# Counts by destination out of the first layer's sums instead of a second histogram

## The reference

```python
x = layernorm(x + segment_sum(x[src], dst, 3125))          # layer 0
x = layernorm(x + ten_steps_of_segment_max(x, w, ...))     # layer 1
# layer 2 needs, for each node, the sum of the weights of its edges, plus one:
deg = segment_sum(concat(edge_weight, ones), concat(edge_dst, arange(n)))
dinv = where(deg > 0, rsqrt(deg), 0)
# layer 3 divides by the number of edges that end in the node:
cnt = segment_sum(ones(E), i_idx); s / maximum(cnt, 1)
```

## Time and profile before

| | us |
|---|---|
| median of 3 runs | 8579.5 |
| the runs | 8568.05, 8579.5, 8579.87 |
| profiled execution, its own time | 8566.12 |
| profiled execution, span of its instructions | 8564.4 |
| DVE busy / PE busy in the span | 6750.9 / 6111.6 |
| mean granted TensorE clock | 0.932 |

### The profile page before, as it was taken

The page is one execution under the profiler, slowest core; times in us unless marked ns, Lnnn a source line. Parts: engine busy times, 40 slices in busy tenths (PEclk is TensorE's granted clock), DMA queues, the critical chain, the costliest instruction groups (busy, mean ns, idle before and its releaser), DMA issues. The chain is left out here.

```text
span 8564.4 us, 139046 instructions
## 1 busy us (share of the span) xinstructions
PE 6111.6 (71%) x42018; PEld 3076.7 (36%) x42018; DVE 6750.9 (79%) x10765; ACT 3629.1 (42%) x4488; POOL 2258.3 (26%) x2014
## 2 busy tenths in 40 slices
PE   2111013878989798888989898989698989656665
PEld 2101012344434343443434343434354545323332
DVE  8999778767889888888889898989787979744443
ACT  0133000224656565555656565656344444233333
POOL 0000000001333333324233332424200000277775
PEclk9999999999999999999999999999899999777777
DMA  2000000886767676666767676767576767311111
GB/s 87 3 0 0 22 5 20 296 286 212 251 211 254 204 244 211 230 227 220 241 214 249 210 251 210 253 204 254 186 285 224 292 225 290 120 22 29 26 29 25
DMA packets 450936, 1460.71 MB, mean 171 GB/s; under 512 B 79869, under 2 KB 115365, under 8 KB 383008
## 3 DMA queue, kind: packets, MB, share of 16 engines
q1 hardware_dynamic: 228922, 1119.71, 38.3%
q10 hardware_dynamic: 157440, 298.89, 9.7%
q0 software_dynamic: 63872, 32.83, 2.2%
HBM read 1159.47 MB, written 291.94 MB: 169 GB/s over the span
## 5 line engine op out<-in xcount | busy, mean ns | idle before, releaser
L1465 PE MATMUL acc<-dst_hot,parts 128*128 128x512 bf16 x11600 | 2936.6, 382 | 336.4 <-issue 321.9
L1524 ACT ACTIVATE parts_out<-acc 96x1024 bf16<-96x1024 f32 x2320 | 2364.6, 1019 | 1722.1 <-PE acc L1476 1712.4
L1340 DVE TENSOR_SCALAR dst_hot<-dst_rows,node_f 128x2048 bf16<-128x2048 int16 x2910 | 2050.9, 739 | 120.2 <-PE acc L1476 109.9
L1428 POOL DMA_INDIRECT group_best<-best_dram,best_row x1250 | 1406.6, 1125 | 2696.1 <-SPq L1391 2401.4
L1465 PEld LDWEIGHTS acc<-dst_hot,parts 128*128 x11600 | 1048.7, 97 | 1547.8 <-issue 665.8
L993 POOL DMA_INDIRECT gathered<-table_dram,source_index x719 | 822.3, 1144 | 1529.5 <-POOLq L158 1310.7
L1476 PE MATMUL acc<-source,parts 128*128 128x128 bf16 x9280 | 910.2, 221 | 118.9 <-DMA source<-source_dram 115.6
L1476 PEld LDWEIGHTS acc<-source,parts 128*128 x9280 | 623.1, 98 | 762.6 <-issue 313.8
L1553 DVE TENSOR_TENSOR_SCAN best<-joined,best,risen 128x512 f32<-128x512 uint8 x570 | 727.6, 1276 | 0.7
L1547 DVE SCALAR_TENSOR_TENSOR risen<-rise,factor 128x512 f32<-128x512 f32 x580 | 400.9, 691 | 377.9 <-PE rise L1488 354.0
L360 PE MATMUL turned<-identity,ping 128*128 128x128 f32 x224 | 55.1, 428 | 771.7 <-DVEq L449 771.7
(11 more groups left out here) (378 smaller groups left out, 8269.9 us busy)
## 6 DMA issues: line engine op xcount, KB each, us to landing
dst_rows<-step_dst_dram SPq DMA_DIRECT2D x291, 1024.0 KB, 4.6
source<-source_dram SPq DMA_DIRECT2D x291, 1024.0 KB, 7.2
dst_kept_in<-dst_hot_dram SPq DMA_DIRECT2D x174, 1280.0 KB, 5.7
best_dram<-best_out ACTq DMA_DIRECT2D x580, 256.0 KB
factor<-step_weight_dram ACTq DMA_DIRECT2D x560, 256.0 KB
sources<-source_dram SPq DMA_DIRECT2D x174, 512.0 KB, 6.6
dst_hot_dram<-dst_kept SPq DMA_DIRECT2D x58, 1280.0 KB, 5.5
src_rows<-step_src_dram SPq DMA_DIRECT2D x58, 512.0 KB, 7.3
```

What stands on the lines that cost most here:

```text
L1340: nc.vector.tensor_scalar(hot[k % 2][b][:, :], index_rows[k // 2 % 2][:, k % 2, :], node_f[:, b:b + 1], None, ALU.is_equal).then_inc(hot_r ...
L1428: pool.indirect_dma_start(group_best[:, g, h, :], None, best_dram, bass.IndirectOffsetOnAxis(ap=best_row[:, i:i + 1], axis=0)).then_inc(en ...
L1465: nc.tensor.matmul(acc[n % 3][:, 0:TILE], blocks[b], hot[k % 2][b][:, q * TILE:(q + 1) * TILE], start=(b == 0), stop=(b == DST_BLOCKS - 1))
L1524: act.activation(moved[n % (2 * QUADS)][:, :], acc[n % 3][0:SPLIT, :], ACT.Copy).then_inc(tile_moved, 1)
```

## The change

The second histogram is taken out, with the matmuls, the weights' parts and the root that belonged to it. Instead `found_first` gets four more columns for each edge slot (`MARKED` = 100): the number 1 and the three bf16 parts of the slot's weight, so that the first layer's sums by destination also hold the count and the weighted sum. DVE builds these columns once for all slots (`marks_col`, from the sorted weights `w_col`) at the start of the first layer; POOL copies the 16x4 columns of a step into `found_first` in each of the 58 steps, and PE waits for that copy at the start of each step's additions (`marked`). The matmuls that turn the sums back have 36 columns for each block instead of 32 (`OUT`), so ACT moves them out in two pieces, one a bank. The root of the weighted sum is taken between that and the normalisation, the two matmuls for the running total follow on PE, and the chain to `end_row` stands in the short phase before the loop.

```diff
+MARKED, OUT = SPLIT + 4, D + 4
...
@@ sort phase, DVE
-                    for i in range(3):
-                        link(V.tensor_copy(w_parts[0:EP, i, :], w_in[0:EP, :]))
-                        link(V.tensor_tensor(w_in[0:EP, :], w_in[0:EP, :], w_parts[0:EP, i, :], ALU.subtract))
...
-                    histogram(1)
-                    link(V.tensor_copy(count[:, :], hist[:, 0:HI]))
...
-                    link(V.tensor_tensor(end_row[1][:, :], t0[:, :], last_at[:, :], ALU.add))
                     read_sources(dve, link, 1, (1,), own_node, tmp, hot_cols, hot_rows, hot_t, cols_ready, cols_turned, index_ready)
...
@@ first layer, POOL
+                    pool.memset(ones_first[:, :], 1.0).then_inc(const_done, 1)
+                    pool.wait_ge(const_done, 2)
+                    pool.affine_select(out=upto_first[:, :], in_=ones_first[:, :], compare_op=ALU.is_ge, fill=0.0,
+                                       base=0, pattern=[[1, P]], channel_multiplier=-1).then_inc(const_done, 1)
+                    pool.wait_ge(marks_ready, 1)
+                    for k in range(STEPS1):
+                        if k >= 2:
+                            pool.wait_ge(added, (k - 1) * STEP_SUBS)
+                        pool.tensor_copy(found[k % 2][:, :, SPLIT:MARKED], marks_col[:, k * STEP_SUBS:(k + 1) * STEP_SUBS, :]).then_inc(marked, 1)
...
@@ first layer, PE
                             if t >= 0:
                                 pe.wait_ge(tile_moved, t + 1)
+                                if not q:
+                                    pe.wait_ge(marked, c + 1)
...
+                        last = nc.tensor.matmul(sums[:, b * BANK + at * OUT:b * BANK + (at + 1) * OUT], flat_first[:, h * P:(h + 1) * P], sum_f[:, :], start=True, stop=True)
...
+                    pe.wait_ge(degree_ready, 1)
+                    nc.tensor.matmul(sums[:, 2 * BANK:2 * BANK + HI], upto_first[:, :], degree[:, :], start=True, stop=True)
+                    nc.tensor.matmul(sums[:, 2 * BANK + HI:2 * BANK + 2 * HI], ones_first[:, :], degree[:, :], start=True, stop=True).then_inc(degree_summed, 1)
...
@@ first layer, ACT
+                    for b in range(2):
+                        h, n = b * (BANK // OUT), min(BANK // OUT, HI - b * (BANK // OUT))
+                        act.activation(node_sums[:, h:h + n, :].rearrange("p h c -> p (h c)"), sums[:, b * BANK:b * BANK + n * OUT], ACT.Copy).then_inc(rows_moved, 1)
+                    act.wait_ge(root_ready, 1)
+                    act.activation(inv_root[:, :], inv_root[:, :], ACT.Sqrt).then_inc(root_done, 1)
...
@@ first layer, DVE
-                    link(V.tensor_copy(sum_f[:, :], sum_parts[:, :]))
+                    link(V.memset(sum_f[:, :], 0.0))
+                    V.tensor_copy(sum_f[0:SPLIT, 0:D], sum_parts[:, :])
+                    link(V.tensor_copy(sum_f[SPLIT:MARKED, D:OUT], identity[SPLIT:MARKED, SPLIT:MARKED]))
+                    V.memset(marks_col[:, :, 0], 1.0)
+                    link(V.tensor_copy(marks_col[:, :, 1], w_col[:, :]))
+                    link(V.tensor_tensor(w_left[:, :], w_col[:, :], marks_col[:, :, 1], ALU.subtract))
+                    link(V.tensor_copy(marks_col[:, :, 2], w_left[:, :]))
+                    link(V.tensor_tensor(marks_col[:, :, 3], w_left[:, :], marks_col[:, :, 2], ALU.subtract))
+                    V.drain().then_inc(marks_ready, 1)
```

More of the change, by code:

```diff
@@ new lines, in _ @@
+                    for n in range(steps):
+                        pe.wait_ge(hot_ready, n + 1)
+                        for f in range(EB):
+                            last = nc.tensor.matmul(hist[:, 0:BUCKETS], one_low[0:EP, n % 2, f, :], one_high[0:EP, n % 2, f, :],
+                                                    start=(n == 0 and f == 0), stop=(n == steps - 1 and f == EB - 1))
+                        last.then_inc(hot_used, 1)
+                    pe.wait_ge(count_ready, 1)
+                    nc.tensor.matmul(sums[:, 0:BUCKETS], upto[:, :], count0[:, :], start=True, stop=True)
@@ new lines, in _, with turn_rows @@
+                    nc.tensor.matmul(sums[:, BUCKETS:2 * BUCKETS], ones[:, :], count0[:, :], start=True, stop=True).then_inc(sums_done, 1)
+                    sort_tensor(pe, turn_ready0, turned_done0, copied0, swapped, load_turned, load_moved)
+                    def turn_rows(to, of):
+                        for i in range(STEP_SUBS):
+                            half, at = divmod(i, STEP_SUBS // 2)
+                            q, j = divmod(i, SUBS)
+                            last = nc.tensor.transpose(to[:, half * BANK + at * STEPS1:half * BANK + (at + 1) * STEPS1],
+                                                       of[:, q, j * P:(j + 1) * P].bitcast(F32), identity[0:STEPS1, 0:STEPS1])
+                        return last
@@ L1113, in one_hot_of @@
                 return dst_hot[(c * len(MADE_SUBS) + MADE_SUBS.index(i)) % HOTS1][:, :]
-            found = [sb(f"found_first{i}", [P, STEP_SUBS, SPLIT], BF16, own) for i in range(2)]
+            found = [sb(f"found_first{i}", [P, STEP_SUBS, MARKED], BF16, own) for i in range(2)]
             identity16 = sb("identity16_first", [P, 2 * BANK], BF16, own)
-            flat_first = sb("flat_first", [SPLIT, NPAD], F32, own)
-            sum_f = sb("sum_f", [SPLIT, D], F32, own)
+            marks_col = sb("marks_col", [P, SUBTILES, 4], BF16, own)
+            w_left = sb("w_left", [P, SUBTILES], F32, own)
+            flat_first = sb("flat_first", [MARKED, NPAD], F32, own)
+            sum_f = sb("sum_f", [MARKED, OUT], F32, own)
+            node_sums = sb("node_sums", [P, HI, OUT], F32, own)
+            upto_first = sb("upto_first", [P, P], F32, own)
+            ones_first = sb("ones_first", [P, P], F32, own)
             sums = own.enter_context(nc.psum_tensor("sums_first", [P, 7 * BANK], F32))
```

173 lines of the change are left out of this document (65 added, 108 removed).

## The result

The changed kernel took 8312.63 us (median of 4 runs, 8309.81 to 8315.25) against 8579.69 us (median of 4, 8568.05 to 8587.33) for the kernel before: ratio 0.969, 95% interval 0.9673 to 0.9707. The profiled execution took 8315.25 us, 251 less than the profiled one of before.

A forecast was written before the change was run, and what follows sets the result against it. DVE alone was taken to bound the second histogram's stretch, transfers to pace the first layer. Terms -243.1 + 2.3 + 0 + 0.5 + 1 + 1 + 0 = -238.3 us from 8573 gave 8335 us, range 8318 to 8362.

The forecast's parts named there:

- The removal: Sort phase, from the cast of `w_parts` to `read_sources`: everything between goes, -243.1 us.
- The root and the degree: Before the normalisation: the chain of small instructions from `count` to `total` returns with DVE alone on the path, +2.3 us.
- The chain to `end_row`: Short phase before the loop: 3.1 us of work fits into DVE's 3.71 us idle time, 0 us, 0.6 to spare.
- The move out: After the first layer's additions: turning matmuls with 36 columns for 32, +0.2 us, and ACT's move, +0.3; together +0.5 us.
- The marks once: Start of the first layer: DVE's mark columns make `source_made` 2.0 us later, PE not delayed; +1 us, between 0 and 2.
- POOL's copies: First layer: 58 copies of 0.2 us each, with PE's wait, mostly absorbed by slack; +1 us, 0 to 12.
- Weight loads: First layer's additions: 100 columns for 96, at most 5 ns more than 127 ns, hidden; 0 us, 0 to 12.
- signs of being wrong: PE waiting for POOL, `found_first` weight loads beyond 135 ns, or DVE's first-layer one-hots longer than 0.39 us.
- The distance to PE's first additions: Start of the first layer: first additions still 13.1 us after the first seeding matmul.
- the rest of the 8564.4 us runs as before: All outside one stretch of the sort phase and one phase after it was taken as unchanged.
- -243 to -213 from either base: Whole kernel: bounds of the change, from the profiled execution's 8566.1 us or the runs' median of 8579.5.
- the case in which the later phases could only lose: Rival, after the first layer: PE's granted clock falls half a percent, half of it shows, +15 us, 8350; chance 0.07.

The follow-up runs named there:

- the removal alone: Kernel before with only the second histogram's 40 steps and input preparation taken out, counts and weighted sums constant: 8317.08 us, ratio 0.9705; with an unused 200-byte tile, 0.9703.
- the doubling: Kernel before with the second histogram's 40 steps done twice, from zero again the second time: 8807.12 us, ratio 1.0268.
- the marks on POOL: Changed kernel with the marks' memset, casts and subtractions on POOL instead of DVE: 8324.61 us, ratio 0.9707; with 256 bytes for the persistent tile, 8331.66 us, 0.9728.

## Why the prediction was right or wrong

The direction and the mechanism of the touched phases were right, the time lay 5 us outside the range, and the failed step is named at the end.

- **The removal, -243.1:** the seed of the first layer starts 241.7 to 243.3 us earlier in the traces of the changed kernel; the removal alone (236.9 us earlier, 237.4 worked out) and the doubling (227 later, 230 worked out) confirm that each step costs its length.
- **The root and the degree, +2.3:** 2.1 measured.
- **The chain to `end_row`, 0:** covered, with 0.35 us left of the 0.6 that were worked out.
- **The move out, +0.5:** ACT's two pieces take 0.98 us against 0.84. The 25 turning matmuls took 9.03 instead of 9.89 us, less and not more. The granted clock accounts for it: in the kernel before it was 1.00 (2.4 GHz) until 1980.3 and 0.50 (1.2 GHz) after, 1.1 us after the matmuls began; in the changed kernel it fell at 1742.2, 2.1 us after they began. PE had been idle for 3.2 us ahead in both. So the distance of 0.198 us that the prediction read is a mean over two levels: 8 of the matmuls came in the first 0.81 us, at 1.00, and 24 in a later 5.00 us, at 0.50.
- **The marks once, +1, between 0 and 2:** mis-sized. `source_made` came 4.7 us later and not 2.0, because a subtraction that reads and writes bf16 with gaps took 2.21 us and not 1.15, and 1.35 us passed before the memset. The 24 seeding matmuls no longer covered it, the granted clock was then 0.50 for 10.2 us instead of 3.4, the first addition came 3.75 us later, and in the end the phase was longer by about 3 us (493.5 to 495.4 against 489.0 to 491.5 us in the traces of the kernel before, from seed to close). With the marks on POOL it was 488.9 and 492.8 us, so this start is what it paid for.
- **POOL's copies, +1:** 0.33 us each in the median (0.2 assumed), and 0 on the path. Here the port rule of the Trainium skill (SBUF — State Buffer, Who interferes with whom) can be weighed: the trace with the marks on POOL agrees with it, a DVE cast of 0.18 us being held for 4.19 us, through two POOL instructions. With short copies in a phase that has slack it changed nothing.
- **Weight loads, 0:** 125 ns, no growth.

These sum to 236 to 238 us at the start of the loop against a forecast of 238.3; that it is so near owes something to luck, since the marks cost 2 us more than taken and the copies 1 us less. Of what the prediction named as signs of being wrong none came: nothing waited for POOL, the loads had 125 ns, DVE's one-hots 0.38 us. The distance to PE's first additions did move, 16.8 us where it said 13.1.

The step that failed is the first sentence of the prediction, that "the rest of the 8564.4 us runs as before", a term put at nothing, and with it the bounds of "-243 to -213 from either base" and the case in which the later phases could only lose. (The bound of -243 also leaves out the +2.3 that the sum counts as certain; by its own terms it would be -241.) They gained 13 us in the first pair of traces and about 20 by the medians. A persistent tile of 200 bytes moved the tiles behind it by 224 bytes, and that alone is worth 22 us on the kernel before; widened to 256 bytes, it takes most of the surplus from the changed kernel. But it is not the whole account: a few us in layer 2 do not follow the shift, and the removal alone gained 16 to 19 us with no shift at all. Also, the base: the profiled execution and the three runs gave 8566 to 8580, and the pooled runs put the kernel at 8573 as assumed, while the runs that the result was measured with stood at 8580.

What stays open: by what mechanism the place of the tiles in SBUF changes the waits in the loop, why the kernel without the histogram is fast at both places, and why the first pass of layer 2 is shorter in some kernels.

## What to carry to other kernels

A part that occupies one engine alone, with no transfer under it, is worth its length, and taking a sum that another phase makes anyway costs a few us of set-up; look at that set-up, for here one subtraction with gaps on both sides took 2.21 us instead of 1.15, and behind the later start the granted clock stood at 0.50 for 10.2 us instead of 3.4. Compare phase by phase and not only the whole: the kernel with the marks on POOL looked like nothing won, and its first layer was 5 us shorter. Then ask what an edit does to the places of the tiles of all later phases: here a 200-byte tile moved the time by 0.26% with not an instruction changed, more than all terms of the sum but the first. When differences of half a percent matter, time the kernel with one or two paddings before crediting them to the edit; for this kernel the range would have needed 20 to 40 us for it.

## What the runs showed of the hardware

- Moving the tiles in SBUF by 224, 256 or 352 bytes a partition changed the time of the kernel before by -21, -3 and +40 us in 8573; the changed kernel lay 18 to 23 us below its sum with 224, 4 below with 256 and 23 above with 288. It does not follow the shift modulo 64, and in the kernel without the histogram 224 bytes changed nothing by the ratio (0.9703 against 0.9705).
- While POOL ran instructions of 2.2 us over 128x928, a DVE cast of 0.18 us took 4.19 us; copies of 0.24 us in the median on POOL, nine in a step, did not lengthen DVE's busy time (345.0 against 345.9 us).
- A DVE subtraction over 128x928 that read and wrote bf16 elements standing eight bytes apart took 2.21 us; one that read such elements and wrote fp32 without gaps took 1.12, and a cast of fp32 into such elements 1.21.
- The granted clock fell from 1.00 to 0.50 at 1980.3 in the kernel before and at 1742.2 in the changed kernel, 1.1 and 2.1 us after fp32 matmuls had begun behind 3.2 us without any; the same 50 took 9.89 and 9.03 us.
